# Latent attention in a two-layer decoder: scores made a second time with keys over the partitions, in place of turning the probabilities

## The chip, the cores and the metric

The kernel runs on one core of a Trainium2 chip. The core has five engines that run side by side and meet only at semaphores: TensorE (PE in the profile; its weight loads are PEld), VectorE (DVE), ScalarE (ACT), GpSimd (POOL) and SyncE (SP), which mostly issues DMAs. Matmuls read SBUF and write PSUM, which has eight banks of 512 float32 per partition. GpSimd works on SBUF here, never on PSUM. The metric is device time of one execution in microseconds (us); lower is better. The whole decoder (two layers) is one program, and the change touches only its first attention.

## What is computed

The part that matters is the self-attention of layer 0, on 2 sequences of 1024 tokens with 256 channels, 16 heads of 16 channels:

```python
q = x @ Wq;  k = x @ Wk;  v = x @ Wv
latent_kv = (k + v) @ W_down_kv              # 64 channels
k_rec, v_rec = latent_kv @ W_up_k, latent_kv @ W_up_v
scores = clip(einsum('bhqd,bhkd->bhqk', qh, kh) / 16, -1e4, 1e4)
scores = clip(scores * exp(-0.0001 * abs(iq - ik)), -1e4, 1e4)
out = einsum('bhqk,bhkd->bhqd', softmax(scores), vh) @ Wo
```

Everything else (a layer norm ahead of each block, cross-attention, a ternary feed-forward block, a linear attention, a second cross-attention and a mixture of experts) stays as it is.

## The kernel before, in words

The program is a row of blocks. Each block gives every engine its list of instructions, and no engine goes on to the next block before all engines and the queues that they fed are through the present one. Two blocks are touched.

`latent_projections` (from L302) makes 16 pieces: for each group of 512 tokens (`g`, four of them) two pieces of queries and two of keys, each 128 channels by 512 tokens. So that bf16 matmuls give float32 scores, each piece is split into three bf16 parts. ScalarE rounds it (L422, first part), VectorE subtracts that (L383, the rest), ScalarE rounds the rest (L429), VectorE subtracts again (L390, third part). VectorE also takes the largest absolute value (L385), from which `k.inside` says whether the clip can be left out. SP stores the three parts to DRAM in one DMA of 384 KB a piece (L445), in `q_parts` and `k_parts`. ScalarE also copies the values to `v_heads` (L433).

`latent_attention` (from L451) goes through 32 pairs of batch and head with 8 query tiles of 128 each, 256 steps in all. SP fetches 12 pieces of 32 KB for each pair (L537, L541) and stacks them to 96 rows: the six products of parts that count, 16 channels each. One step is, for 128 queries:

- TensorE makes the scores of 128 queries by 1024 keys, two matmuls (L578).
- VectorE multiplies them with the fading, writes `probs` and takes the row's peak, in one instruction (L659).
- GpSimd turns the peak's sign (L563), and ScalarE takes the exponential with that as bias and sums the row (L706).
- TensorE turns the 128 x 1024 probabilities, eight transposes (L588), since the product with the values wants keys over the partitions; ScalarE copies three of each four halves out of PSUM (L521), VectorE the fourth (L519).
- TensorE sums over the values (L603): every four steps 64 matmuls of 128 columns, four query tiles side by side in the four column groups of 32. A short chain (L695, L612, L637, L640) turns the result back and divides it by the row sum.

The order is written out by hand: `step` on each engine says what it does in step `s`, with the transposes three steps (`LAG`) and the sums up to eight steps (`TRAIL`) behind. The two score tiles of PSUM banks 0 to 3 alternate, banks 4 and 5 take the transposes, bank 6 the sums, bank 7 what is turned back. The engines run this in loops with registers (`Fori`). At the end of its list GpSimd clears the slots of the mixture of experts: a memset and one DMA of 5031 KB to DRAM (L114, L116).

`cross_attention` (from L733), which is not changed, already works with keys over the partitions, and its rows are used below: scores twice (L826 for the peaks, L851 for the exponential), the peak taken off by a matmul with rows of minus one (L857), the sum over the values with 512 moving columns in four column groups (L871).

## Time and profile before

| | us |
|---|---|
| median of 3 runs | 1614.19 |
| lowest and highest of them | 1610.89, 1617.33 |
| the profiled execution, its own time | 1615.76 |
| its span, first to last instruction | 1614.2 |
| busy in the span: PE, DVE, ACT, POOL | 1340.0, 919.8, 930.1, 190.5 |

The profiled execution is 0.1% above the median. Rows below have their stage or line with them. A row of the timeline gives the start in us, how long the row's instructions took together, the engine, the line and operation, and in brackets how long the engine was idle ahead of it and what released it. Two instructions that follow each other overlap in their latency, so the step from one start to the next is the price of one in a stream, and the mean duration of one is more than that. The granted clock of TensorE is given as a share of 2.4 GHz: 1.00 is the higher of its two levels, 0.50 the lower (1.2 GHz).

### The profile page before, as it was taken

The numbers are of one execution on the slowest core, as the hardware profiler recorded it, in microseconds if no ns is written. First come the engines' busy times: TensorE is split into PE (matmuls) and PEld (weight loads), VectorE is DVE, ScalarE is ACT, GpSimd is POOL, SyncE is SP. The second block draws the span as 40 slices with busy tenths as digits, with TensorE's granted clock in tenths as the row PEclk, the third lists the DMA queues.
The fourth block names the chain that finished last, engine by engine and source line by source line (L and its number), as shares of the span: only waits on it lengthen the run. The fifth ranks groups of instructions, "written<-read, shape, count | busy, mean of one in ns | idle before, by whom it ended". The sixth has DMA issues, their size and how long they took to land. (4 is left out here: it accounts for less than half of the span.)

```text
span 1614.2 us, 36474 instructions
## 1 busy us (share of the span) xinstructions
PE 1340.0 (83%) x12288; PEld 960.2 (59%) x12291; DVE 919.8 (57%) x2059; ACT 930.1 (58%) x1793; POOL 190.5 (12%) x546
## 2 busy tenths in 40 slices
PE   5879999999999995898365699889874489999992
PEld 2347777777777774544223464364354279999992
DVE  5558888888888873532788844563354223323233
ACT  2469999999999991355375377624631033333330
POOL 0001111111111110111200000031120701111110
PEclk9879999999999997899756899988995589999996
DMA  3311010010101013200000100033006211111115
GB/s 115 131 51 31 22 27 24 24 26 23 29 20 29 20 38 110 80 1 4 16 1 0 31 1 1 1 120 129 1 4 212 102 34 36 37 36 38 36 33 166
DMA packets 60025, 74.30 MB, mean 46 GB/s; under 512 B 13006, under 2 KB 47728, under 8 KB 59952
## 3 DMA queue, kind: packets, MB, share of 16 engines
q1 hardware_dynamic: 53168, 56.76, 11.9%
q0 software_dynamic: 4672, 14.50, 2.7%
q10 hardware_dynamic: 2112, 2.10, 0.4%
q8 instruction: 43, 0.70, 0.2%
q14 instruction: 30, 0.25, 0.0%
HBM read 50.43 MB, written 22.88 MB: 45 GB/s over the span
## 5 line engine op out<-in xcount | busy, mean ns | idle before, releaser
L659 DVE CUSTOM_DVE_ANT_0 probs_sb<-banks,decay_sb 128x1024 f32<-128x1024 f32 x256 | 308.2, 1221 | 43.6 <-PE banks L578 22.5
L706 ACT ACTIVATE probs_sb<-probs_sb,shift_sb 128x1024 f32<-128x1024 f32 x256 | 294.8, 1151 | 18.1 <-POOL shift_sb L563 16.4
L588 PEld LDWEIGHTS banks<-ident_sb,probs_sb 128*128 128x128 f32 x2048 | 238.3, 141 | 55.1 <-issue 22.9
L588 PE MATMUL banks<-ident_sb,probs_sb 128*128 128x128 f32 x2048 | 267.8, 274 | 0.9 <-ACT probs_t_sb L521 0.8
L521 ACT ACTIVATE probs_t_sb<-banks 128x512 f32<-128x512 f32 x384 | 214.7, 597 | 4.1 <-PE banks L588 2.3
L578 PE MATMUL banks<-k_stack_sb,q_stack_sb 96*128 96x512 bf16 x512 | 156.9, 389 | 14.0 <-DMA k_stack_sb<-k_parts 10.7
L603 PE MATMUL banks<-probs_t_sb,v_head_sb 128*32 128x128 f32 x4096 | 151.2, 277 | 0.7 <-ACT probs_t_sb L521 0.7
L1846 PEld LDWEIGHTS banks<-slots_xt_sb,tile_w_sb 128*128 128x128 f32 x1248 | 146.5, 193 | 1.9
L1846 PE MATMUL banks<-slots_xt_sb,tile_w_sb 128*128 128x128 f32 x1248 | 146.6, 276 | 0.0
L1858 PE MATMUL banks<-experts_w_sb,xt_sb 128*128 x624 | 141.2, 379 | 1.3 <-issue 1.3
L1892 ACT ACTIVATE slots_xt_sb<-banks 128x256 f32<-128x256 f32 x39 | 14.9, 383 | 213.8 <-PE banks L1832 213.8
L1858 PEld LDWEIGHTS banks<-experts_w_sb,xt_sb 128*128 128x128 f32 x624 | 115.5, 190 | 15.8 <-issue 1.7
L519 DVE COPY probs_t_sb<-banks 128x512 f32<-128x512 f32 x128 | 88.6, 692 | 57.7 <-PE banks L588 56.0
L603 PEld LDWEIGHTS banks<-probs_t_sb,v_head_sb 128*32 128x32 f32 x4096 | 100.3, 109 | 32.3 <-issue 31.4
L563 POOL TENSOR_TENSOR shift_sb<-peak_sb,minus_sb 128x1 f32<-128x1 f32 x256 | 48.5, 190 | 452.8 <-DVE peak_sb L659 452.8
L977 DVE TENSOR_REDUCE peak_sb<-banks 128x8 f32<-128x616 f32 x64 | 49.9, 798 | 87.8 <-PE banks L826 87.8
L1019 ACT ACTIVATE pt_sb<-banks,keyfill_sb 77x1024 f32<-77x1024 f32 x64 | 67.5, 1104 | 38.0 <-PE banks L857 37.1
L1902 ACT ACTIVATE xt_sb<-banks,tile_b_sb 128x128 f32<-128x128 f32 x312 | 84.7, 387 | 5.1 <-PE banks L1846 3.4
L1942 DVE COPY tile_w_sb<-experts_w_sb 128x2048 f32 x39 | 47.8, 1227 | 60.2 <-issue 28.0
L1927 DVE TENSOR_TENSOR is_best_sb<-slots_x_sb,tile_owned_sb 128x1 f32<-128x1 f32 x39 | 6.2, 159 | 122.2 <-DMA outputs_y<-slots_y_sb,output_row_sb 122.2
L253 POOL TENSOR_TENSOR x_sb<-x_sb,bb_sb 128x256 f32<-128x256 f32 x48 | 33.0, 732 | 337.2 <-DMA bb_sb<-in_L_attn_bo 276.7
L1881 POOL DMA_INDIRECT outputs_y<-slots_y_sb,output_row_sb x39 | 37.4, 959 | 258.7 <-DVE slots_y_sb L1955 154.0
(289 smaller groups left out, 1910.0 us busy)
## 6 DMA issues: line engine op xcount, KB each, us to landing
experts_w_sb<-in_L_ffn_W SPq DMA_DIRECT2D x16, 1024.0 KB, 11.9
q_stack_sb<-q_parts SPq DMA_DIRECT2D x192, 32.0 KB, 1.7
k_stack_sb<-k_parts SPq DMA_DIRECT2D x192, 32.0 KB, 1.8
slots_x<-zeros_sb POOLq DMA_DIRECT2D x1, 5031.0 KB, 22.6
slots_x_sb<-slots_x SPq DMA_DIRECT2D x39, 129.0 KB, 2.1
xt_sb<-outputs_y SPq DMA_DIRECT2D x8, 512.0 KB, 5.5
q_parts<-parts_sb SPq DMA_DIRECT2D x8, 384.0 KB, 3.0
k_parts<-parts_sb SPq DMA_DIRECT2D x8, 384.0 KB, 4.2
```

The source lines that it names most:

```text
L519: ins = eng.tensor_copy(dst, k.ps[:, 4 + half, :])
L521: ins = eng.activation(dst, k.ps[:, 4 + half, :], ACT.Copy)
L578: last = pe.matmul(k.ps[:, 2 * (s % 2) + half, :], qs[:, u, q * P:(q + 1) * P], ks[:, u, half * 512:(half + 1) * 512], start=True, stop=True)
L588: last = pe.transpose(k.ps[:, 4 + half, j * P:(j + 1) * P], pr[:, s % 4, (half * TPG + j) * P:(half * TPG + j + 1) * P], k.ident[:, :])
L603: last = pe.matmul(k.ps[32 * j:32 * j + 32, 6, 0:P], vh[:, u, kt, :], pt[:, j, gs % 2, kt, :], start=kt == 0, stop=kt == QT - 1)
L659: dve.tensor_tensor_reduce(out=pr[:, s % 4, :], in0=scores, in1=decay[:, off:off + S], scale=1.0, scalar=-3.0e38, op0=ALU.mult, op1=ALU.ma ...
L706: act.activation(pr[:, s % 4, :], pr[:, s % 4, :], ACT.Exp, bias=shift[:, s % 8:s % 8 + 1], accum_out=sums[:, (s // TPG) % 4, s % 4:s % 4 ...
L977: dve.tensor_reduce(peak[:, t % TPG, 2 * half:2 * half + 2, :], k.ps[:, bank:bank + 2, 0:SLOTS * C].rearrange("p r (s n) -> p r s n", n=C) ...
L1019: act.activation(pt[:, n % 2, 2 * half:2 * half + 2, :], k.ps[0:C, 2 * half:2 * half + 2, :], ACT.Exp, bias=key_fill[:, b:b + 1]).then_inc ...
L1846: last = pe.matmul(k.ps[:, 2 * u + f // HALF, (f % HALF) * P:(f % HALF + 1) * P], w1[:, u, kd, f * P:(f + 1) * P], xst[:, u, kd, :], start ...
L1858: last = pe.matmul(k.ps[:, 6, s * D:(s + 1) * D], ht[:, s, f, :], r.w2[:, bass.ds(e, 1), f, :].rearrange("p a n -> p (a n)"), start=f == 0 ...
L1902: ins = act.activation(ht[:, s, f, :], k.ps[:, 2 * s + f // HALF, (f % HALF) * P:(f % HALF + 1) * P], ACT.Gelu_apprx_tanh, bias=b1[:, s, f ...
```

## The change

In the projections every query and key piece is made in two versions: multiplied along the token with exp(-0.0001 i) or exp(+0.0001 i), and the second version negated twice (the sign is in both queries and keys). The fading exp(-0.0001 |i - j|) is then part of the product: one version holds for keys up to the query, the other for keys after it. So there are 32 pieces to split and store where there were 16, the fading being one VectorE instruction with the maximum in it; the third part moves to GpSimd. The value matmuls go behind the queries of the next group, and the queries of group 0 ahead of the latent weights. Six slots hold parts where there were four. Two fade tables (512 KB each), a second table `inner` beside `decay` and rows of minus one are fetched by DMA in this block.

The stacks in SBUF are laid out anew: channel c of piece x lies on partition 6c + x, and four heads are fetched by one DMA (6 of 128 KB of queries for every group, 6 of 256 KB of keys for every second). Rows 96 to 98 of the key stack are minus one, and those of the query stack get the peaks, in three bf16 parts, by DMA.

The attention goes through 16 groups of 4 heads by 512 queries. Each group has 16 tiles of 128 queries by 1024 keys, whose scores serve only for the peak (VectorE, one instruction a tile, result thrown away), and 8 steps over tiles of 128 keys. A step makes for each of the four heads the scores of 128 keys by 512 queries with the peak taken off, and ScalarE takes their exponential from PSUM into the layout that the sum over values wants. Where a key tile lies on the diagonal (4 of 8 steps) a fifth unit makes the four diagonal blocks in the other version, and GpSimd zeroes in both what does not hold (`affine_select`, two a step). The sum over values follows two steps behind. The row sum comes from a column of ones in `v_head`. The transposes, their copies, the sign on GpSimd and the loops with registers are gone; the order is unrolled.

```diff
-                for half in range(2):
-                    last = pe.matmul(k.ps[:, 2 * (s % 2) + half, :], qs[:, u, q * P:(q + 1) * P],
-                                     ks[:, u, half * 512:(half + 1) * 512], start=True, stop=True)
+                for version in range(2):
+                    for half in range(2):
+                        lo, hi = max(half * G, 0 if version == 0 else edge), min((half + 1) * G, edge if version == 0 else S)
+                        if lo < hi:
+                            last = pe.matmul(k.ps[:, 2 * (tile % 2) + half, lo - half * G:hi - half * G],
+                                             stacks.q[0:ROWS, g % 3, version, h, j * P:(j + 1) * P],
+                                             stacks.k[0:ROWS, g // 2 % 2, version, h, lo:hi], start=True, stop=True)
...
+            def key_product(g, i, h, bank, version, lo, hi, at):
+                kt = key_tile(g, i)
+                return pe.matmul(k.ps[:, bank, at:at + hi - lo],
+                                 stacks.k[0:ROWS + PARTS, g // 2 % 2, version, h, kt * P:(kt + 1) * P],
+                                 stacks.q[0:ROWS + PARTS, g % 3, version, h, lo:hi], start=True, stop=True)
...
-            def turn(i, s):
...
+                if on_diagonal(i):
+                    pe.wait_ge(selected, s // 2 + 1)
+                    lo = block_of(g, i) * P
+                    for h in range(HEADS):
+                        pe.matmul(k.ps[VW * h:VW * (h + 1), PV_BANK, lo:lo + P], vh[:, n % 2, h, kt, :],
+                                  probs_d[:, s // 2 % 2, h, :], start=False, stop=False, skip_group_check=True)
+                for h in range(HEADS):
+                    last = pe.matmul(k.ps[VW * h:VW * (h + 1), PV_BANK, :], vh[:, n % 2, h, kt, :], probs_of(s)[:, h, :],
+                                     start=i == 0, stop=i == QT - 1, skip_group_check=True)
...
+            for tile in range(TILES + LEAD):
+                scores(tile)
+                if tile == TILES + 1:
+                    turn_peaks(0)
+            for g in range(GROUPS):
+                for i in range(QT):
+                    if g * QT + i >= 2:
+                        sum_values(g * QT + i - 2)
+                    for x in range(2):
+                        for h in range(2 * x, 2 * x + 2):
+                            key_scores(g, i, h)
+                        if x == 1 and i == TURN_STEP and g + 1 < GROUPS:
+                            turn_peaks(g + 1)
+                        if tile_at(g, i, x) < GROUPS * TILES:
+                            scores(tile_at(g, i, x))
+                    if on_diagonal(i):
+                        diagonal_scores(g, i)
+                    if i == 3 and g > 0:
+                        turn_mix(g - 1)
...
+                pool.wait_ge(exp_done, unit_index(g, i, HEADS - 1) + 1)
+                pool.affine_select(later, later, [[0, HEADS], [1, P]], ALU.is_ge, 0.0, base=0, channel_multiplier=-1)
+                earlier = probs_d[:, s // 2 % 2, :, :]
+                pool.wait_ge(exp_done, unit_index(g, i, HEADS) + 1)
+                pool.affine_select(earlier, earlier, [[0, HEADS], [-1, P]], ALU.is_gt, 0.0, base=0,
+                                   channel_multiplier=1).then_inc(selected, 1)
...
+            def exponential(g, i, h):
+                u, s = unit_index(g, i, h), g * QT + i
+                act.wait_ge(key_scored, u + 1)
+                act.wait_ge(released, u + 1)
+                if h == 0:
+                    wait(act, summed, s - 2)
...
+                act.activation(out, k.ps[:, bank_of((exp_done, u + 1)), :], ACT.Exp).then_inc(exp_done, 1)
```

The key scores, the turned peaks and what is turned back share banks 4 to 6 in a ring (`bank_of`, `wait_for_bank`): an item waits until the third before it has been read. `LEAD` is 6, `TILES` 16, `TURN_STEP` 5, `UNITS` 36 a group, so that 22 tiles go ahead of the first key scores. In the projections:

```diff
+                dve.tensor_tensor_reduce(out=rest[:, e % 4, :], in0=k.ps[:, n % 4, :], in1=fade[:, side, half * G:(half + 1) * G],
+                                         scale=sign * (scale if is_query(e) else 1.0), scalar=-3.0e38, op0=ALU.mult, op1=ALU.max,
+                                         accum_out=extremes[:, version, n:n + 1]).then_inc(faded, 1)
+            def subtract_first(e):
+                dve.wait_ge(part1_done, e + 1)
+                dve.tensor_tensor(rest[:, e % 4, :], rest[:, e % 4, :], parts[:, e % SLOTS, 0, :],
+                                  ALU.subtract).then_inc(rest1_done, 1)
...
+        @block.gpsimd
+        def _(pool):
+            for e in range(NV):
+                pool.wait_ge(part2_done, e + 1)
+                pool.wait_ge(rest1_done, e + 1)
+                pool.tensor_tensor(parts[:, e % SLOTS, 2, :], rest[:, e % 4, :], parts[:, e % SLOTS, 1, :],
+                                   ALU.subtract).then_inc(part3_done, 1)
```

`clear_slots` stays the last thing on GpSimd's list in the attention.

## Rows read from the trace of the kernel before

**Rows 1.** Busy time by stage: projections, attention.
```profile
core 0: us, PE busy (x) PEld busy (x) DVE busy (x) ACT busy (x) POOL busy (x), PEclk, DMA share, GB/s
22.50:84.00 61.50, 48.26 (x106) 20.25 (x106) 31.61 (x55) 25.43 (x53) 0.00 (x0) 0.81 0.31 103
84.00:621.50 537.50, 510.11 (x6720) 375.91 (x6720) 412.60 (x768) 498.26 (x961) 59.75 (x292) 0.97 0.13 33
```

**Rows 2.** Groups of instructions in the attention: busy us, mean ns, idle before.
```profile
L706 ACT ACTIVATE probs_sb<-probs_sb,shift_sb 128x1024 f32<-128x1024 f32 x256 | 294.8, 1151 | 18.1 <-POOL shift_sb L563 16.4
L521 ACT ACTIVATE probs_t_sb<-banks 128x512 f32<-128x512 f32 x384 | 214.7, 597 | 4.1 <-PE banks L588 2.3
```

**Rows 3.** Timeline of the attention's end, DVE, PE and POOL.
```profile
607.51 0.22 DVE L640 TENSOR_TENSOR attn_sb<-banks,inv_sb 128x64 f32<-128x64 f32 x1 [3.04 <-PE banks L612]
622.23 0.45 PE L261 MATMUL banks<-ident_sb,attn_sb 128*128 128x128 f32 x1 [14.82 <-PEq L475]
...
599.24 2.22 POOL L116 DMA_DIRECT2D slots_x<-zeros_sb  x1 [0.32 <-POOL zeros_sb L114]
```

**Rows 4.** DMA issues: size and median us from issue to landing.
```profile
slots_x<-zeros_sb POOLq DMA_DIRECT2D x1, 5031.0 KB, 22.6
q_stack_sb<-q_parts SPq DMA_DIRECT2D x192, 32.0 KB, 1.7
f_b_sb<-in_L_ffn_b SPq DMA_DIRECT2D x1, 512.0 KB, 3.4
```

**Rows 5.** Groups of instructions in the projections.
```profile
L383 DVE SCALAR_TENSOR_TENSOR rest_sb<-banks,parts_sb 128x512 f32<-128x512 f32 x16 | 11.0, 686 | 22.0 <-ACT parts_sb L422 22.0
L429 ACT ACTIVATE parts_sb<-rest_sb 128x512 bf16<-128x512 f32 x16 | 8.7, 617 | 0.0
```

**Rows 6.** GpSimd elementwise groups anywhere in the program.
```profile
L253 POOL TENSOR_TENSOR x_sb<-x_sb,bb_sb 128x256 f32<-128x256 f32 x48 | 33.0, 732 | 337.2 <-DMA bb_sb<-in_L_attn_bo 276.7 <-DMA bb_sb<-in_L_xattn_bo 60.5
L563 POOL TENSOR_TENSOR shift_sb<-peak_sb,minus_sb 128x1 f32<-128x1 f32 x256 | 48.5, 190 | 452.8 <-DVE peak_sb L659 452.8
L559 POOL COPY v_head_sb<-v_heads_sb 128x128 f32<-128x128 f32 x4 | 1.2, 289 | 0.1
L548 POOL MEMSET v_head_sb<- 128x512 f32 x1 | 0.5, 524 | 84.9 <-issue 84.9
```

**Rows 7.** The stretch of 40 to 44 us: DMA at full load, stores of four pieces.
```profile
40.00:44.00 4.00, 4.00 (x7) 2.13 (x8) 0.50 (x1) 0.82 (x3) 0.00 (x0) 0.50 1.03 340
```

**Rows 8.** Timeline of the attention's start.
```profile
85.33 0.52 POOL L548 MEMSET v_head_sb<- 128x512 f32 x1 [84.88 <-issue]
90.91 1.89 PE L578 MATMUL banks<-k_stack_sb,q_stack_sb 96*128 96x512 bf16 x4 [10.71 <-DMA k_stack_sb<-k_parts]
92.11 1.23 DVE L659 CUSTOM_DVE_ANT_0 probs_sb<-banks,decay_sb 128x1024 f32<-128x1024 f32 x1 [11.11 <-PE banks L578]
93.26 1.22 DVE L659 CUSTOM_DVE_ANT_0 probs_sb<-banks,decay_sb 128x1024 f32<-128x1024 f32 x1
```

**Rows 9.** PE's timeline over one and a half steps in mid-attention.
```profile
303.35 0.60 PE L578 MATMUL banks<-k_stack_sb,q_stack_sb 96*128 96x512 bf16 x2
303.78 1.04 PE L588 MATMUL banks<-ident_sb,probs_sb 128*128 128x128 f32 x8
304.75 0.86 PE L603 MATMUL banks<-probs_t_sb,v_head_sb 128*32 128x128 f32 x24
305.55 0.60 PE L578 MATMUL banks<-k_stack_sb,q_stack_sb 96*128 96x512 bf16 x2
```

**Rows 10.** Timeline of the first cross-attention: value sum and exponentials.
```profile
685.59 1.07 PE L871 MATMUL banks<-pt_sb,va_sb 77*32 77x512 f32 x8
691.01 2.11 ACT L1019 ACTIVATE pt_sb<-banks,keyfill_sb 77x1024 f32<-77x1024 f32 x2 [0.48 <-PE banks L857]
```

**Rows 11.** PE's clock while the attention gets going.
```profile
99.00:100.00 1.00, 1.00 (x6) 0.80 (x5) 1.00 (x2) 0.52 (x2) 0.00 (x0) 0.50 0.00 0
100.00:200.00 100.00, 98.94 (x1286) 73.11 (x1284) 80.59 (x149) 97.11 (x188) 11.03 (x56) 1.00 0.10 25
```

More of the change, by code:

```diff
@@ L341, in latent, with values @@
                 last.then_inc(lat_ready, 1)
-            latent(0)
+            def values(g, m):
+                for t in range(g * TPG + 2 * m, g * TPG + 2 * m + 2):
+                    wait(pe, v_done, t - 1)
+                    pe.matmul(k.ps[:, 5 + t % 2, 0:D], lat[:, t * P:(t + 1) * P], k.wuv[:, :],
+                              start=True, stop=True).then_inc(v_ready, 1)
             for g in range(NG):
@@ L347, in _ @@
                     n = 4 * g + m
[L348 removed]
+                    if g > 0:
+                        values(g - 1, m)
+                    wait(pe, faded, 2 * (n - 3))
                     for kd in range(KD):
@@ L360, in _ @@
                     latent(g + 1)
[L361 to L365 removed]
+            for m in range(KD):
+                values(NG - 1, m)
             pe.wait_ge(largest_ready, 1)
@@ L440, in _ @@
+            later.start(sp)
+            for e in range(NV):
+                n, version = divmod(e, 2)
                 g, s = divmod(n, 4)
@@ new lines, in _, with load_stacks @@
+                if 20 <= e < 26:
+                    load_stacks(sp, stacks, 0, e - 20)
+            for x in range(SLOTS):
+                sp.wait_ge(stored[x], 16 * len(range(x, NV, SLOTS)))
+            later.wait(sp)
+class Stacks:
+    pass
+HEADS = 4
+def load_stacks(eng, stacks, g, piece):
+    n, half = divmod(g, 2)
+    b, first = divmod(n * HEADS, H)
+    rows = slice(b * D + first * HD, b * D + (first + HEADS) * HD)
+    q_part, k_part = [(0, 0), (0, 1), (0, 2), (1, 0), (1, 1), (2, 0)][piece]
+    dst = slice(piece, 6 * HD, 6)
+    if half == 0:
+        eng.dma_start(stacks.k[dst, n % 2, :, :, :].rearrange("p v h n -> p v (h n)"),
+                      stacks.k_scratch[:, k_part, rows, :].rearrange("v (p h) n -> p v (h n)", h=HEADS)
+                      ).then_inc(stacks.arrived[g % 3], 16)
+    eng.dma_start(stacks.q[dst, g % 3, :, :, :].rearrange("p v h n -> p v (h n)"),
+                  stacks.q_scratch[:, q_part, half, rows, :].rearrange("v (p h) n -> p v (h n)", h=HEADS)
+                  ).then_inc(stacks.arrived[g % 3], 16)
@@ new lines, in _ @@
+            own.wait()
+            stage_values(0)
+            split_peaks(0)
+            for g in range(GROUPS):
+                for i in range(QT):
+                    if on_diagonal(i):
+                        select(g, i)
+                    if i == 3 and g % 2 == 0 and g + 2 < GROUPS:
+                        stage_values(g // 2 + 1)
+                    if i == TURN_STEP - 1 and g + 1 < GROUPS:
+                        split_peaks(g + 1)
+            clear_slots(k, pool, zeros_set)
```

662 lines of the change are left out of this document (384 added, 278 removed).

## The prediction

> **What bounds it now.** I read the busy time by stage first. The attention takes 537.5 us of the span, the projections ahead of it 61.5. In the attention PE shows 510 us busy, ACT 498, DVE 413 [rows 1]. PE's figure overstates: its rows hold latency, and two score matmuls that show 0.60 us together are followed 0.43 later by the next ones [rows 9], so some 0.17 of each row is latency. The groups then say what ACT does for one step: an exponential of 1024 columns (1.15) and one and a half copies of 512 (0.60 each) [rows 2]: 2.05 us. The 256 steps go from 90.9 to 607.5 [rows 3, 8], 2.02 us each. So ACT sets the pace, and what the change takes from it is the copies.
>
> The timeline of the end shows something else. The last VectorE result of the attention starts at 607.5, and the next block's first matmul at 622.2. GpSimd has issued the clearing DMA at 599.2, which takes 22.6 us [rows 3, 4]: it lands at 621.8. The block cannot end before GpSimd's queue is through, so 14.8 us are idle, and the attention's end is "GpSimd's list is done, plus 22.6 + 0.6". That decides what the new order is worth.
>
> **Projections.** Removed: 16 absolute maxima on DVE. Added: 16 more pieces. For each of the 32, DVE does one multiply-reduce from PSUM and one subtraction, 0.69 each in the row of L383, some 0.6 in a stream: 1.25 us. ACT does two roundings (0.62 each, about 0.55 in a stream) plus values, about 1.3 us [rows 5]. GpSimd's third part is not in the trace at this size. 256 columns with two inputs take 0.73, one column 0.19 [rows 6], hence (0.73 - 0.19) x 2 + 0.19 = 1.27 for 512; the ends are 0.52 (the memset of 512) and 1.46 (twice the 256). It waits for ACT each time, another 0.16 or so. I take the upper end, 1.46 + 0.16 = 1.62 us a piece, since it is GpSimd's only two-input rate here; 32 x 1.62 = 52 us. Fade tables of 512 KB take 3.4 to land [rows 4], so the first piece starts at about 26.5 (22.5 + two issues + 3.4); with 5 us for the last piece and its store the block ends at 83. DMA is close behind: 32 x 384 KB, 1024 + 2016 KB of tables and 2304 KB of the first stacks are 18.1 MB, at the 340 GB/s of a full stretch [rows 7] 53 us. The reorder of values and queries hides under both. So the attention starts at 84, as now. Cover gone: each 0.1 us a piece is 3 us.
>
> **Lead.** GpSimd, from 85.3, first clears 2048 columns (four times 0.52) and copies the identity (0.29) [rows 6, 8], and PE waits for that: first tile at 87.7. Nothing waits for stacks, which now costs 7 us (first matmul at 90.9 though SP starts fetching at 84) [rows 8]. Then 22 tiles pass before the first key scores. VectorE paces them: 1.15 from start to start [rows 8]. The matmuls of tile 21 wait for the reduction of tile 19, at 88.9 + 20 x 1.15 = 111.9. The peaks of group 0 are complete at 107.3, need four small GpSimd steps (0.2 to 0.3 each with their waits), a turn and copy (1.0) and a small DMA (1.7 plus issue), about 111.7: equal. First key scores at 112.3; today the first probabilities come at 93.6. This is a cost of 19 us.
>
> **Main part.** Two steps (one diagonal) are the unit, 64 of them. PE:
> - Value sums: 8 matmuls of 512 columns in column groups take 1.07 with latency [rows 10], 0.90 without. Going in and out costs more: 303.78 + (1.04 - 0.17) is 304.65 and L603 starts at 304.75; 304.75 + 0.69 is 305.44 and L578 starts at 305.55 [rows 9]. So 0.90 + 0.21, twice: 2.22.
> - Diagonal sums: 8 of 128 columns, a third of 0.69: 0.23.
> - Key scores: 8 x 512 columns at 0.215 [rows 9]: 1.72. The three rows more on the contracting side I take as free, since the price is by moving columns in every row here.
> - Peak tiles: 4 x 0.43 = 1.72. Diagonal scores: 512 columns in four matmuls, 0.24. Six matmuls cut in two at the edge: 0.02 each, 0.12.
> - Sum 6.25; 0.05 for the ring of three banks makes 6.3.
>
> Once a group come the turned peaks and four transposes, 0.6 x 16 = 9.6 us; the last 11 steps have no tiles, 22 x 0.43 = 9.5 back. They cancel.
>
> ACT: 9 exponentials of 512. Half of the 1024-column pair's 2.11 / 2 is 0.53 [rows 10], the 512 copy is 0.60 [rows 2]; 0.57 x 9 + 0.25 for peaks and mix = 5.4. DVE: 4 x 1.15 + 0.2 = 4.8. PE becomes the bound, at 6.3 per pair against today's 2.02 x 4 = 8.1 for the same 4 tiles. Low end 5.6 (gaps and ring hidden, ACT next), high end 7.1 (below).
>
> The selects stand on PE's way: the diagonal sum waits for them. By laying out the pair, the fourth exponential of a diagonal step ends at 3.8 us, both selects at 3.8 + 2d + 0.1, and PE wants the result at 5.9; so nothing up to d = 1.0 us, then 2d - 2.0 a pair. The trace has no select. Nearest is the strided copy: 128 columns 0.29, so (0.29 - 0.10) x 4 + 0.10 = 0.86 for 512; the ends are 0.52 (memset) and 1.46 (two inputs) [rows 6]. I take 0.86, no wait; 1.46 would add 0.9 a pair, hence 7.1.
>
> The Trainium skill (GPSIMD Engine Reference, "Elementwise — side-by-side cycle accounting") gives a loop of one input about 1.0 to 1.8 cycles an element, 2.6 with two inputs. By it a select of 512 would be about 0.4 to 0.8 us plus dispatch, an estimate, and would not stall; no run here shows one.
>
> Stacks: 2304 KB every second group, asked for at its start, wanted 5 steps (15.7 us) later; at 340 GB/s 7 us plus 12 issues. Hidden. The queue of SP holds nothing that they delay but the peak rows, wanted three steps later.
>
> PE is at 0.50 through the lead, as it still is at 99 to 100 today [rows 11]; 3 us for the climb. Main part: 64 x 6.3 + 3 = 406, so PE's last diagonal product is at 518.
>
> **Tail.** Exponential and latency 1.0, second select 0.9, then memset and start 0.6 and the DMA's 22.6, 0.3 to the next block: 25.4, so the next block starts at 543.7 instead of 622.2. The remaining sums, about 4 us, lie under that DMA. It is 19 us of idle time instead of 14.8.
>
> **Sum.** Against the profiled 1615.8: -78.5, gives 1537.3; against the median (1614.2) 1536. I say 1537.
>
> **Rivals.**
> 1. *The drains and the ring cost nothing, ACT sets the pace.* 5.6 a pair: 64 x 0.7 = 45 less, 1492. For: from the scores to L588 (303.35 to 303.78) there is no gap. Against: L603 has one of 0.1 on either side [rows 9], and the change keeps its column groups.
> 2. *GpSimd and VectorE exclude each other in the projections.* If the third part (two SBUF inputs) and VectorE's subtraction (two SBUF inputs) take turns, a piece costs 1.62 + 0.69 = 2.31, 32 x 0.69 = 22 us more: 1559. The trace has no such pair of operations together, so it speaks neither way. The Trainium skill (SBUF — State Buffer, "SBUF: two separate sides") states exactly this lock: one blocks the other for a whole instruction.
> 3. *The select is the bound; the one on the other side.* Above 1.0 us each select pushes the diagonal sum, with all of PE's list behind it. At 1.46: 58 us more, 1595. No gain is left at 2d - 2.0 = 78.5 / 64, d = 1.61; slower than before by over 0.5% (1624) from d = 1.68. For: a select also computes an index and a comparison for every element. Against: it has one input, like the copy.
> 4. *The clipped path runs*, because the bound got stricter by exp(-0.2) = 0.82. Over 2000 VectorE instructions more of some 0.6 us: above 2500. The trace shows L659 reading the banks directly [rows 8], which is the unclipped form, with scores of order one against 10000. Practically excluded.
>
> **Chances.** Forecast 0.50 (range of its own 1515 to 1555), rival 1 0.15, rival 2 0.17, a select between 1.0 and 1.6 us 0.08, one at break-even 0.02, slower 0.08. Range 1490 to 1595: from rival 1 to the high end of the select. Half a per cent (8 us) is about what measurement tells from no change. Faster 0.90, same 0.02, slower 0.08.
>
> **What would show it.** PE steps of 3.0 to 3.3 us with small ACT gaps; no L588 and no copies of L521. The multiply-reduce of the peaks at 1.15 in the lead and spaced afterwards. First exponential near 112. GpSimd selects near 0.9 us, and PE's sum never waiting for them. Projections of 32 pieces at 1.6, ending at 83. PE idle for about 19 us at the end under the 22.6 us DMA. Wrong would be: an attention paced by GpSimd, a wait of PE for the stacks at the sixth step of even groups, or pieces above 2 us.

## The result

| | us |
|---|---|
| kernel before, median of 4 runs on the same chip | 1614.64 (1610.89 to 1617.33) |
| kernel after, median of 4 runs | 1557.85 (1553.99 to 1560.41) |
| ratio, 95% interval | 0.9648, 0.9617 to 0.9679 |
| profiled execution of after: own time, span | 1560.41, 1558.3 |

Forecast were 1537 and 1490 to 1595. The time lies in that range but above the forecast's own range of 1515 to 1555. The program became 3.5% faster, 71% of what was forecast: 55.4 us between the two profiled executions where I had 78.5.

**Stages of after** [rows 1], here with the lead as a stage of its own: projections, lead, main part.

```profile
22.50:95.50 73.00, 48.47 (x106) 18.15 (x104) 49.13 (x103) 43.84 (x84) 46.42 (x32) 0.78 0.74 248
95.50:127.00 31.50, 23.12 (x64) 5.91 (x65) 25.13 (x43) 1.56 (x2) 3.81 (x8) 0.50 0.41 101
127.00:538.00 411.00, 400.33 (x3185) 163.04 (x3184) 289.52 (x500) 305.24 (x603) 95.13 (x193) 0.99 0.21 50
```

The projections take 73 us where they took 61.5. In the main part PE is busy for 97% of the time at a clock of 0.99, ACT for 74%, DVE for 70%. ACT's copies are gone, and the bound has moved to PE.

**PE, ACT and DVE in mid-attention** [rows 9], the weight loads left out:

```profile
303.82 0.60 PE L654 MATMUL banks<-q_stack_sb,k_stack_sb 99*128 99x512 bf16 x2
...
304.16 1.23 DVE L816 CUSTOM_DVE_ANT_0 faded_scores_sb<-banks,inner_sb 128x1024 f32<-128x1024 f32 x1 [0.96 <-PE banks L647]
304.26 0.60 PE L647 MATMUL banks<-k_stack_sb,q_stack_sb 96*128 96x512 bf16 x2
...
304.78 0.43 PE L692 MATMUL banks<-probs_d_sb,v_head_sb 128*32 128x128 f32 x8
...
305.02 1.04 PE L695 MATMUL banks<-probs_sb,v_head_sb 128*32 128x512 f32 x8
...
306.00 0.61 PE L654 MATMUL banks<-q_stack_sb,k_stack_sb 99*128 99x384 bf16 x4
...
306.43 1.08 ACT L915 ACTIVATE xt_sb<-banks 128x512 f32<-128x512 f32 x2 [0.99 <-PE banks L654]
```

DVE and ACT both wait about 1 us for PE, once a step; PE has no wait in brackets; over the whole main part its waits come to 8 us. Two score matmuls that start at 304.26 should be through 0.43 later, at 304.69, and L692 starts at 304.78. L695 starts at 305.02, has 0.87 of columns, and L654 follows at 306.00 instead of 305.89. These are the gaps of 0.09 and 0.11 around work in column groups. The next L692 is at 310.91, so a pair of steps takes 6.13 us.

**Groups that carry the attention and the projections** [rows 2, 5, 6]: busy us, mean ns, idle before.

```profile
L915 ACT ACTIVATE xt_sb<-banks 128x512 f32<-128x512 f32 x342 | 178.0, 604 | 73.4 <-PE banks L654 73.4
L775 POOL TENSOR_SCALAR_AFFINE_SELECT probs_d_sb<-probs_d_sb 128x512 f32<-128x512 f32 x63 | 40.0, 634 | 2.2 <-ACT probs_d_sb L915 2.0
L703 PE MATMUL banks<-ident_b_sb,peak_parts_sb 128*96 128x128 bf16 x15 | 3.9, 257 | 4.7 <-POOL peak_parts_sb L764 4.7
...
L439 POOL TENSOR_TENSOR parts_sb<-rest_sb,parts_sb 128x512 bf16<-128x512 f32 x32 | 46.4, 1477 | 44.3 <-ACT parts_sb L455 44.2
L405 DVE TENSOR_TENSOR rest_sb<-rest_sb,parts_sb 128x512 f32<-128x512 f32 x32 | 29.4, 919 | 8.2 <-ACT parts_sb L451 8.1
L399 DVE CUSTOM_DVE_ANT_0 rest_sb<-banks,fade_sb 128x512 f32<-128x512 f32 x32 | 21.7, 681 | 10.8 <-DMA fade_sb<-in_c_fade 5.5 <-PE banks L376 5.3
```

L405 is the same subtraction as L383 before, which took 686 ns; here its mean is 919.

**The attention's start and end** [rows 3, 8]:

```profile
99.06 0.29 POOL L744 CAST ident_b_sb<-ident_sb 128x128 bf16<-128x128 f32 x1
...
99.41 1.89 PE L647 MATMUL banks<-k_stack_sb,q_stack_sb 96*128 96x128 bf16 x6 [9.38 <-POOL ident_b_sb L744]
...
100.59 1.23 DVE L816 CUSTOM_DVE_ANT_0 faded_scores_sb<-banks,inner_sb 128x1024 f32<-128x1024 f32 x1 [9.17 <-PE banks L647]
...
539.99 0.63 POOL L775 TENSOR_SCALAR_AFFINE_SELECT probs_d_sb<-probs_d_sb 128x512 f32<-128x512 f32 x1
540.57 0.31 POOL L114 MEMSET zeros_sb<- 128x258 f32 x1
540.77 0.42 PE L692 MATMUL banks<-probs_d_sb,v_head_sb 128*32 128x128 f32 x8 [0.97 <-POOL probs_d_sb L775]
...
541.20 2.23 POOL L116 DMA_DIRECT2D slots_x<-zeros_sb  x1 [0.32 <-POOL zeros_sb L114]
...
543.75 0.43 DVE L800 TENSOR_TENSOR attn_sb<-banks,inv_sb 128x256 f32<-128x256 f32 x1
563.38 3.01 PE L261 MATMUL banks<-ident_sb,attn_sb 128*128 128x128 f32 x13 [19.96 <-PEq L590]
```

DVE has its last result at 544.2, and the next block begins at 563.4, after 19 us under the clearing DMA.

**DMA issues** [rows 4]:

```profile
k_stack_sb<-k_parts SPq DMA_DIRECT2D x48, 256.0 KB, 4.9
q_stack_sb<-q_parts SPq DMA_DIRECT2D x96, 128.0 KB, 3.4
...
slots_x<-zeros_sb POOLq DMA_DIRECT2D x1, 5031.0 KB, 21.8
```

So the 58.8 us by which the next block begins earlier (622.2 before) are made of a first key or score product 35.5 later (90.9 to 126.4), 104.4 less from there to the last diagonal product or DVE result (516.6 to 412.2), and 10.1 more of tail (14.7 to 24.8). The rest of the program, the same code, took 3.5 us longer in this execution. That ACT set the pace before is read from its rows [rows 1, 2]; no run changes the copies alone.

### The profile page after: what moved, and what is told of

Its sections match the earlier page's. It is cut to its first block and busy times, and to the rows that moved or that the text cites. A ratio compares the mean times of both kernels' runs of the same rounds, so it can differ in the third digit from the quotient of the medians.

```text
span 1558.3 us, 26085 instructions
## 1 busy us (share of the span) xinstructions
PE 1257.4 (81%) x8850; PEld 752.1 (48%) x8851; DVE 840.2 (54%) x1883; ACT 759.1 (49%) x1473; POOL 279.8 (18%) x491
## 2 busy tenths in 40 slices
DMA packets 63104, 96.09 MB, mean 62 GB/s; under 512 B 11057, under 2 KB 51923, under 8 KB 61459
## 3 DMA queue, kind: packets, MB, share of 16 engines
q1 hardware_dynamic: 56214, 78.14, 17.1%
## 5 line engine op out<-in xcount | busy, mean ns | idle before, releaser
L816 DVE CUSTOM_DVE_ANT_0 faded_scores_sb<-banks,inner_sb 128x1024 f32<-128x1024 f32 x256 | 304.5, 1223 | 102.2 <-PE banks L647 101.1
L915 ACT ACTIVATE xt_sb<-banks 128x512 f32<-128x512 f32 x344 | 179.0, 604 | 73.4 <-PE banks L654 73.4
L654 PE MATMUL banks<-q_stack_sb,k_stack_sb 99*128 99x128 bf16 (+3 forms) x960 | 181.0, 297 | 5.8 <-ACT xt_sb L915 2.6
L647 PE MATMUL banks<-k_stack_sb,q_stack_sb 96*128 96x512 bf16 (+3 forms) x704 | 163.9, 339 | 13.7 <-POOL ident_b_sb L744 9.4
L654 PEld LDWEIGHTS banks<-q_stack_sb,k_stack_sb 99*128 99x128 bf16 x960 | 71.7, 97 | 158.9 <-ACT xt_sb L915 66.6
L915 ACT ACTIVATE probs_sb<-banks 128x512 f32<-128x512 f32 x168 | 87.3, 605 | 34.2 <-PE banks L654 34.2
L647 PEld LDWEIGHTS banks<-k_stack_sb,q_stack_sb 96*128 96x128 bf16 x704 | 66.0, 101 | 75.8 <-DVE peak_sb L816 16.8
L695 PE MATMUL banks<-xt_sb,v_head_sb 128*32 128x512 f32 x688 | 90.6, 598 | 0.0
L772 POOL TENSOR_SCALAR_AFFINE_SELECT xt_sb<-xt_sb 128x512 f32<-128x512 f32 x43 | 27.3, 635 | 182.0 <-ACT xt_sb L915 182.0
L293 DVE TENSOR_TENSOR x_sb<-x_sb,banks 128x256 f32<-128x256 f32 x64 | 26.9, 421 | 52.6 <-PE banks L275 35.8
```

What stands on the lines that cost most here:

```text
L647: last = pe.matmul(k.ps[:, 2 * (tile % 2) + half, lo - half * G:hi - half * G], stacks.q[0:ROWS, g % 3, version, h, j * P:(j + 1) * P], st ...
L654: return pe.matmul(k.ps[:, bank, at:at + hi - lo], stacks.k[0:ROWS + PARTS, g // 2 % 2, version, h, kt * P:(kt + 1) * P], stacks.q[0:ROWS ...
L695: last = pe.matmul(k.ps[VW * h:VW * (h + 1), PV_BANK, :], vh[:, n % 2, h, kt, :], probs_of(s)[:, h, :], start=i == 0, stop=i == QT - 1, sk ...
L816: dve.tensor_tensor_reduce(out=junk[:, tile % 2, :], in0=tile_scores(tile), in1=inner[:, window(tile)], scale=1.0, scalar=-3.0e38, op0=ALU ...
L915: act.activation(out, k.ps[:, bank_of((exp_done, u + 1)), :], ACT.Exp).then_inc(exp_done, 1)
```

## The experiments

Twelve kernels ran, each against the kernel before on the same chip. Times in brackets are the lowest and highest, the ratio is to the kernel before. They ran on four chips, where the median of the kernel before was 1611.83, 1612.66, 1612.93 and 1615.62 us, and after ran beside 1614.64. A difference from after of 2 or 3 us can therefore be the chip's, and the ratios decide.

**Where the tail goes.** On the kernel after, the slots are cleared behind group 8.

```diff
+                if g == CLEAR_GROUP:
+                    clear_slots(k, pool, zeros_set)
-            clear_slots(k, pool, zeros_set)
```

> The changed kernel with clear_slots issued after group 8 of the 16, not at the end of GpSimd's list. Theory A (the attention block ends when GpSimd's 5031 KB DMA has landed): the 19.6 us from the last VectorE result (544.2) to the next block's first matmul (563.4) shrink to 1 to 2 us, less one pause of 2.2 us at most in the middle: 1538 to 1541 us. Rival (the block's end waits for something else, or the DMA in the middle slows the fetches of the stacks so that TensorE waits for them): 1550 or more, or a wait for the stacks of several us in groups 9 and 10.

Measured: 1544.07 us (1543.21 to 1547.2), ratio 0.9585 [0.9564, 0.9606], 13.8 less than after, and 10 less by the ratios: above theory's 1538 to 1541, well below the rival's 1550. In the trace the next block begins 16.3 earlier:

```profile
543.83 0.42 DVE L802 TENSOR_TENSOR attn_sb<-banks,inv_sb 128x256 f32<-128x256 f32 x1
547.05 2.37 PE L261 MATMUL banks<-ident_sb,attn_sb 128*128 128x128 f32 x10 [3.55 <-PEq L591]
```

The 19 us are 2.8, and the DMA beside the groups slows none of them: every group from the third to the thirteenth takes 26.02 us, as in after. The same edit on the kernel before, with the clearing behind the first pass:

```diff
-            bodies(pool, body)
+            body(0, True, False)
             clear_slots(k, pool, zeros_set)
+            with pool.Fori(1, NB - 1) as i:
+                body(i, False, False)
+            body(NB - 1, False, True)
```

> The kernel before with the same move: clear_slots after the first unrolled pass (step 16) instead of at the end. Theory A: the 14.8 us of idle time at the attention's end go, and GpSimd's 2.2 us of issuing delay the sign of one peak once: 1600 to 1603 us. The difference of the two kernels without the tail is then 60 to 63 us, against 57 with it. Rival: the DMA collides with the small stack fetches in the loop: over 1608.

Measured: 1602.95 us (1602.46 to 1603.73), ratio 0.9947 [0.993, 0.9965]. That lies in theory's 1600 to 1603, but against 1611.83 on this chip it is 8.9 less, where 14.8 less a pause of 2.2 was expected. In the trace the next block begins 12.5 earlier (609.75), after 3.0 us idle. Without either tail the two kernels differ by 58.9 us, with both by 56.8; 60 to 63 was expected.

**Is the select near PE's path?** Every select is done twice.

```diff
+                own.did(pool.affine_select(later, later, [[0, HEADS], [1, P]], ALU.is_ge, 0.0, base=0, channel_multiplier=-1))
+                own.wait()
                 pool.affine_select(later, later, [[0, HEADS], [1, P]], ALU.is_ge, 0.0, base=0, channel_multiplier=-1)
...
```

> The changed kernel with every affine_select on GpSimd done twice (the second changes nothing). One select took 0.635 us here, so two count as d = 1.27 to 1.35 with the wait between. Theory (the layout of the prediction: free up to d = 1.0, then 2d - 2.0 a pair of steps): 0.55 to 0.7 us a pair, 64 pairs, 35 to 45 us more: 1593 to 1603. Rival (more slack than laid out, since the sum over a diagonal tile follows a whole step later and TensorE is the bound): under 15 us more. Other rival (GpSimd's selects slow VectorE or ScalarE by themselves): more than 60, with longer single operations.

Measured: 1574.51 us (1573.78 to 1579.92), ratio 0.9781 [0.9756, 0.9806]; theory's 1593 to 1603 is missed, and the rival's limit of 15 more is passed by little. The main part, first exponential to last key product, went from 410.8 to 429.3 us: 18.5 more, 0.29 a pair. From start to start a doubled select takes 1.29, and my layout of the pair gives 2 x 1.29 - 2.0 = 0.58, 37 us. So the rule "free up to 1.0, then twice the excess" is too strict: if its slope holds, which one point can't show, the free part ends at 1.15. As the select takes 0.635 there is room of some 0.5 us for each, and it costs nothing. The stalls are in half of the pairs only, in PE's waits (us in total, times, longest):

```profile
PE banks L692 <- POOL probs_d_sb L780: 15.9, 33, 1.0
```

**The extra step of a group.** A group of 8 steps takes 26.02 us where 8 x 3.07 are 24.56. One of the steps with extras is the one that turns the next group's peaks (3.62), where PE waits 0.31 for GpSimd. First, split and turn both go one step later.

```diff
-    TURN_STEP = 5
+    TURN_STEP = 6
```

> The changed kernel with TURN_STEP 6 for 5: the peaks of the next group are split and turned one step later. In the profile a group takes 26.02 us against 8 x 3.07 = 24.56; 0.54 of the excess is TensorE's wait for the split peaks in the sixth step. Theory B: that wait goes, 15 x 0.5 = 7 to 8 us less: 1550. Rival: the peak rows then arrive too late at the next group's first key scores (turn, copy and DMA of about 3 us in 2 steps), so the wait only moves: 1556 to 1560 or more.

Measured: 1558.09 us (1555.53 to 1559.09), ratio 0.9671 [0.9654, 0.9688], as the rival said. PE still waits, 0.37 us now, and the step takes 3.71. The wait had only moved along, since GpSimd's split had moved too. Then the turn alone goes later, and the split stays:

```diff
-    TURN_STEP = 5
+    TURN_STEP = 6
...
-                    if i == TURN_STEP - 1 and g + 1 < GROUPS:
+                    if i == TURN_STEP - 2 and g + 1 < GROUPS:
                         split_peaks(g + 1)
```

> Against the kernel after: GpSimd still splits the peaks of the next group after step 4, TensorE turns them one step later (6 instead of 5). In the earlier run with both moved, TensorE still waited 0.37 us for GpSimd in that step. Theory: the wait of 0.31 us and what hangs on it (the step at 3.62 instead of 3.07) is GpSimd's chain of four small operations behind the last tile's peak; a step of distance takes all of it: the step goes from 3.6 to 3.1 to 3.3, 15 groups by 0.3 to 0.5 are 5 to 8 us, time 1550 to 1553. Rival: what the step costs is the turn itself (four transposes, a bank of the ring held, a copy), so it only moves to the next step: 1557 to 1559, spacings as before in another place.

Measured: 1554.31 us (1550.65 to 1557.83), ratio 0.9634 [0.9614, 0.9655], an interval that overlaps that of after, between theory (1550 to 1553) and rival (1557 to 1559). PE at the turn:

```profile
278.29 0.23 PE L703 MATMUL banks<-ident_b_sb,peak_parts_sb 128*96 128x128 bf16 x1 [0.18 <-ACT xt_sb L915]
```

GpSimd's chain is off the path; in its place comes 0.18 of wait for ACT, which must empty the bank of the ring that the turn wants. The main part is 2.6 us shorter, 0.17 a group: the step goes from 3.62 to 3.49, not to 3.1. So the bulk of the 0.54 is the turn itself and its bank, which this run does not separate.

**The first pieces.** PE waits for the latent weights from 26.5 to 31.8, since DVE copies them only behind two pieces, and those wait for the fade tables. The copy goes ahead of that wait.

```diff
+            dve.wait_ge(wkv_ready, 1)
+            dve.tensor_copy(wkv[:, :, :], k.ps[:, 7, 0:KD * L]...).then_inc(wkv_done, 1)
             dve.wait_ge(fade_arrived, 2 * 16)
...
```

> The changed kernel, where VectorE copies the combined latent weights (0.28 us) ahead of its wait for the fade tables, not after its third fade. In the profile TensorE sits idle from 26.5 to 31.8 for that copy, and VectorE later waits 5.3 us for the first keys and ACT 3.8 for the first values. Theory C: the attention starts 4 to 8 us earlier (at 88 to 92 for 95.5): 1550 to 1554. Rival (the block ends with the DMA traffic, 18 MB at 340 GB/s, which runs at full load from 76 to 92 whatever the start): start at 94 or later, no gain beyond 1.5 us.

Measured: 1556.29 us (1556.11 to 1559.65), ratio 0.9662 [0.9635, 0.9689], not told from after; theory's 1550 to 1554 is missed. The trace's next block starts 2.5 us earlier. PE's wait of 5.3 us for the weights is gone, but its first key product now waits 5.4 us for ACT's copy of the latent, which stands behind the fourth piece on ACT's list.

**GpSimd against VectorE.** The third part goes back to VectorE.

```diff
+            def subtract_second(e):
+                dve.wait_ge(part2_done, e + 1)
+                dve.tensor_tensor(parts[:, e % SLOTS, 2, :], rest[:, e % 4, :], parts[:, e % SLOTS, 1, :],
+                                  ALU.subtract).then_inc(part3_done, 1)
...
-        @block.gpsimd
...
```

> The changed kernel with the third part subtracted on VectorE as in the kernel before, not on GpSimd. In the profile VectorE's subtraction of two SBUF inputs took 1.03 us beside a GpSimd subtraction and 0.69 when alone, GpSimd's 1.48 beside it and 1.15 alone; a piece took 1.57. Theory D (the two share access to SBUF): the subtractions on VectorE are back at 0.69 in every row, and a piece takes 0.61 + 0.60 + 0.60 = 1.8 to 1.9: the start of the attention moves by 0 to +8 us. Rival (VectorE's rows were long for another reason, such as waiting for parts): they stay near 1.03 for the first subtraction, and a piece takes 2.2 or more.

Measured: 1559.65 us (1559.01 to 1561.67), ratio 0.9678 [0.9652, 0.9704]. VectorE's two subtractions a piece:

```profile
L405 DVE TENSOR_TENSOR rest_sb<-rest_sb,parts_sb 128x512 f32<-128x512 f32 x32 | 21.9, 683 | 0.6 <-ACT parts_sb L450 0.5
L410 DVE TENSOR_TENSOR parts_sb<-rest_sb,parts_sb 128x512 bf16<-128x512 f32 x32 | 21.8, 681 | 0.1
```

Alone, the subtraction is at 683 ns again instead of 919, so the conflict is real. In after the two engines' subtractions look like this, in the steady part and at the end, where they hardly overlap:

```profile
52.77 1.04 DVE L405 TENSOR_TENSOR rest_sb<-rest_sb,parts_sb 128x512 f32<-128x512 f32 x1
53.22 1.60 POOL L439 TENSOR_TENSOR parts_sb<-rest_sb,parts_sb 128x512 bf16<-128x512 f32 x1
54.34 1.04 DVE L405 TENSOR_TENSOR rest_sb<-rest_sb,parts_sb 128x512 f32<-128x512 f32 x1
...
81.62 0.69 DVE L405 TENSOR_TENSOR rest_sb<-rest_sb,parts_sb 128x512 f32<-128x512 f32 x1 [0.58 <-ACT parts_sb L451]
82.18 1.15 POOL L439 TENSOR_TENSOR parts_sb<-rest_sb,parts_sb 128x512 bf16<-128x512 f32 x1 [0.74 <-ACT parts_sb L455]
```

That fits two engines that take turns. VectorE alone has a price of 0.61 from start to start; GpSimd's 1.15 less the 0.19 of an operation on one column [rows 6] leaves 0.96 for the elements; together 1.57, an estimate from these rows, and a piece takes 1.57. The rows overlap all the same, as a row is longer than its price in a stream (0.69 for 0.61). No run separates this from a slowdown of another kind.

What GpSimd's help is worth, the medians don't tell. VectorE alone makes a piece in 1.81 us (from 43.1 to 68.5 us), as theory said, and with the help in 1.57. That is 0.25 a piece. But the trace of this run had luck with PE's clock while the pipe filled (below, at the step that failed), and after had not. Beside the three traces with the third part on GpSimd and the same luck, `select_twice`, `turn_step_6` and `rows_two_halves`, VectorE's last piece begins 4.6 to 7.4 us later (87.26 for 79.83 to 82.68), and GpSimd's first memset of the attention comes 2.7 to 5.7 later (98.23 for 92.53 to 95.52).

**The first stacks.** They are fetched in the attention and not beside the last pieces.

```diff
-                if e == 19:
-                    for x in range(SLOTS):
-                        sp.wait_ge(stored[x], 16 * len(range(x, 16, SLOTS)))
-                if 20 <= e < 26:
-                    load_stacks(sp, stacks, 0, e - 20)
...
-            for g in range(1, 3):
+            for g in range(3):
```

> The changed kernel with the first group's stacks fetched at the start of the attention, not between the stores of the projections. Theory E (the end of the projections is bound by DMA: the stores and 2304 KB of fetches share the queue from 72 on, and pieces take 2.3 us instead of 1.57 from 78 to 91): the projections end 6 to 8 us earlier, and the fetch, now in the open, costs about 9: near 0, 1555 to 1562. Rival (the slow pieces at the end have another cause): the projections end where they do, at 91 to 95, and the fetch adds 7 to 9 us: 1564 or more.

Measured: 1564.28 us (1561.85 to 1566.54), ratio 0.97 [0.9674, 0.9726]. GpSimd's first memset of the attention comes at 94.6 instead of 97.2, so without the fetches the projections are 2.6 shorter, but the first tile waits for the stacks until 106.7. Theory's 6 to 8 us did not come out, and the time is the rival's. Both edits together:

> Against the kernel after: the latent weights are copied ahead of the wait for the fade tables, and the first group's stacks are fetched in the attention. Singly the first shortened the projections by 2.4 us of the 5.3 that VectorE had waited (DMA was full from 72 to 88), the second brought GpSimd's first memset of the attention from 97.2 to 94.6. Theory: the copy's gain was lost to the DMA queue, so without the stack fetches the whole 5 us come out: memset at 89 to 90.5, first tile some 12 us behind it, time 1558 to 1561 (5 less than with stacks late alone, 1564.3). Rival: the pace of the 32 pieces on GpSimd and VectorE ends the block either way: memset at 92.5 or later, 1562 to 1565.

Measured: 1564.38 us (1560.4 to 1565.4), ratio 0.969 [0.9674, 0.9706]; the memset is at 91.85, 2.7 earlier than with stacks late alone, where theory said 5 and the rival 2. Of these, 1.1 lie ahead of the block, whose first matmul comes at 21.86 instead of 23.01. The medians do not show even the rest. The copy therefore did not lose its gain to DMA. What took the place of the wait is seen in VectorE's list:

```profile
36.20 0.69 DVE L399 CUSTOM_DVE_ANT_0 rest_sb<-banks,fade_sb 128x512 f32<-128x512 f32 x1 [3.44 <-PE banks L376]
...
43.41 0.69 DVE L405 TENSOR_TENSOR rest_sb<-rest_sb,parts_sb 128x512 f32<-128x512 f32 x1 [4.08 <-ACT parts_sb L450]
```

and among the waits of this kernel (us in total, times, longest):

```profile
PE banks L376 <- ACT lat_sb L445: 5.3, 1, 5.3
...
ACT v_heads_sb L459 <- PE banks L355: 4.3, 1, 4.3
```

PE's key product now waits for ACT's copy of the latent, which stands behind the fourth piece on ACT's list (`e == 3`); and ACT stands at a copy of values with the next roundings behind it. The order of the lists makes the hole, not the one copy; and PE's clock was at 0.50 from 34 to 42 us.

**Rows of the stack.** A piece of 16 channels is put on 16 neighbouring partitions instead of six apart; all else stays.

```diff
-    dst = slice(piece, 6 * HD, 6)
+    dst = slice(piece * HD, (piece + 1) * HD)
```

> The changed kernel without the interleaving: each of the six pieces lies on 16 partitions in a row (piece x on 16x to 16x + 15), everything else as it is. Theory F (a fetch of 128 or 256 KB is spread by its source rows, and what it costs lies under the 15 us that a group leaves): landing within 1 us of 3.4 and 4.9, total within 3 us of 1558. Rival (16 neighbouring partitions share few ports into SBUF): landing times 1.5 to 2 times as long, the fetches of an even group take over 15 us, and TensorE waits for stacks in 7 groups: 1575 or more.

Measured: 1610.03 us (1607.76 to 1614.93), ratio 0.9989 [0.9975, 1.0003]. The whole gain is gone. DMA issues of this kernel, and its main wait from 130 to 580 us (total, times, longest):

```profile
k_stack_sb<-k_parts SPq DMA_DIRECT2D x48, 256.0 KB, 11.7
q_stack_sb<-q_parts SPq DMA_DIRECT2D x96, 128.0 KB, 5.6
```

```profile
PE banks L647 <- DMA q_stack_sb<-q_parts: 30.3, 6, 6.0
```

The busy time by stretch of one set of stacks (the last three columns: PE's clock, DMA share, GB/s):

```profile
192.00:196.00 4.00, 3.85 (x35) 1.53 (x38) 3.32 (x7) 3.01 (x7) 0.00 (x0) 1.00 1.10 121
...
208.00:212.00 4.00, 0.21 (x2) 0.21 (x3) 0.00 (x0) 0.00 (x0) 0.15 (x1) 0.95 0.36 37
212.00:216.00 4.00, 4.00 (x23) 1.96 (x21) 2.42 (x4) 1.84 (x4) 0.87 (x2) 0.50 0.02 5
```

The DMA engines are fully busy at 116 to 121 GB/s; in after the same stretch moves 201 to 240. A set of 2304 KB takes about 21 us instead of 12, and PE wants it 18 us after it is asked for. PE's stand of 5 us also takes the clock to 0.50 for the 4 us after it. The first tile is 11 us later, the main part 44 longer, 30 of them in the waits shown. A version between the two, three apart in two halves of 48 partitions:

```diff
+    dst = slice(piece // 3 * 3 * HD + piece % 3, (piece // 3 + 1) * 3 * HD, 3)
```

> The channels of a piece lie 3 partitions apart, pieces 0 to 2 on partitions 0 to 47 and pieces 3 to 5 on 48 to 95, instead of 6 apart over all 96. Landing of a 256 KB piece of keys was 4.9 us with 6 apart and 11.7 with 16 neighbouring partitions. Theory: the landing goes by how far the 16 rows are spread over the partitions, so it is in between, 6 to 9 us; all 2304 KB of a pair of groups are then through in time or just so, and the program takes 1556 to 1575. Rival one: any spacing is enough (no neighbours in a piece): 4.9 us and 1556 to 1560. Rival two: what counts is that all six pieces share the same partitions, so that a transfer reaches everywhere: landing 10 us or more and 1590 or above.

Measured: 1559.19 us (1555.81 to 1561.83), ratio 0.9673 [0.9659, 0.9688]:

```profile
k_stack_sb<-k_parts SPq DMA_DIRECT2D x48, 256.0 KB, 7.8
```

Landing goes 4.9, 7.8, 11.7 with 96, 48 and 16 partitions reached. These medians hold the wait behind the transfers ahead: on 16 partitions the first of a set's six key pieces lands in 4.6 us and the last in 17.1. The middle layout is still hidden. The Trainium skill (SBUF — State Buffer, "Door 1: The DMA port swizzle (why `[64,N]` ≈ `[32,N]`)") counts for this the ports that a transfer's partitions reach: by its table 13 or 14 with six apart, 8 or 12 with three apart, and 4 for 16 neighbours. The order agrees, and its 104 GB/s for partitions 0 to 15 is near the 116 to 121 here; ports as such no run here shows.

**A version that beats both.** The early clearing, the copy first, the later turn, and PE's wait for the identity moved from the first tile to the first turn:

```diff
-            pe.wait_ge(constants, 1)
             for tile in range(TILES + LEAD):
                 scores(tile)
                 if tile == TILES + 1:
+                    pe.wait_ge(constants, 1)
...
```

> Four edits together on the kernel after: the slots are cleared behind group 8 instead of at the end, the latent weights are copied ahead of the wait for the fade tables, TensorE waits for the identity only where it first turns peaks, and the peaks are turned one step after they are split. Singly: clearing early 1544; the copy about -2; the wait for the identity 1.5 to 2.5 at the first tile; the turn 0 or 5 to 8. Theory: they add up, 1532 to 1541. Rival: the head of the attention is set by when the DMA queue is through, so that only clearing and turn count: 1537 to 1545.

Measured: 1535.25 us (1532.21 to 1536.85), ratio 0.9518 [0.9504, 0.9532]; its interval and that of the early clearing alone (0.9564 to 0.9606) do not meet. Theory's sum, 1532 to 1541, holds.

```profile
94.52 1.87 PE L647 MATMUL banks<-k_stack_sb,q_stack_sb 96*128 96x128 bf16 x6 [6.77 <-PEq L322]
```

First tile at 94.5, main part 408.3 us, next block at 539.6. Of the 23.8 us that the next block is earlier than in after, the tail gives 16.4 and the main part 2.5; the other 4.9 lie at the first tile. The wait for the identity explains 3.8 of them: in this trace it is ready at 98.3, and PE starts at 94.5 with the block's first fetch, where in after it started 3.85 behind it. The rest is not told from chance: with no edit in the projections' order the first tile came anywhere from 94.75 to 100.81 in six of these profiles.

## Why the prediction came out 20 us low

Right in its main lines: ACT's copies bounded before, the change takes them off, PE becomes the bound, and GpSimd's DMA ends the block. The next block was forecast at 543.7 and came at 563.4. By the steps:

- **Projections, 84 against 95.6: the step that failed.** "The reorder of values and queries hides under both" was false. The rate came out nearly right, 1.57 a piece against 1.62, but by luck: GpSimd's subtraction is 1.15 alone and not 1.46, and what makes up for it is the conflict with VectorE, which the forecast left to a rival. But the first 5 pieces needed 18.5 us instead of 8.1. I had priced every instruction and never laid out who waits for whom while the pipe fills: the fade tables hold DVE's list, which holds the latent weights, hence the latent, the keys and the values.

```profile
38.38 0.69 DVE L399 CUSTOM_DVE_ANT_0 rest_sb<-banks,fade_sb 128x512 f32<-128x512 f32 x1 [5.29 <-PE banks L376]
...
45.05 0.69 DVE L405 TENSOR_TENSOR rest_sb<-rest_sb,parts_sb 128x512 f32<-128x512 f32 x1 [3.54 <-ACT parts_sb L451]
```

  These two waits of DVE in after are 8.8 of the 11.6. The whole sum: the first piece is 1.7 late (28.2), the first five cost 10.4 more, 0.6 pass before the sixth, the steady rate gives 1.6 back, the last five take 1.7 more since the stores meet the stack fetches (3.9 us of ACT waiting for stores; DMA share 1.05 from 80 to 88), and from the last piece to the block's end it is 4.3 us instead of the 5.7 that the forecast left.

  A part of it is PE's clock, which the forecast had at nothing here. PE stands still from 26.5 to 31.8, the clock falls to 0.50 and stays there to 43, and PE's list of the latent, the keys, the next latent and the values, all ahead of ACT's copy of values, runs at half speed. In `select_twice`, with the same projections, it was back at 1.00 by 36. The second latent in after, and in `select_twice`:

```profile
39.84 3.61 PE L348 MATMUL banks<-xt_sb,wkv_sb 128*64 128x512 f32 x4
...
38.08 1.93 PE L348 MATMUL banks<-xt_sb,wkv_sb 128*64 128x512 f32 x4
```

  From the first latent to the next queries PE takes 12.7 us in after and 9.2 in `select_twice`, and DVE's two waits are 8.83 and 5.35. So 3.5 of the 11.6 are the clock, beside an execution where it rose early. Three of the six profiles went each way: 99.41 to 100.81 at the first tile with the late rise (after, `clear_mid`, `peaks_turned_later`), 94.75 to 97.74 with the early one. What decides between them no run shows. With the early rise the fetches still begin at 90.9 to 93.9 instead of 84, so the waits on the lists remain the larger part.
- **Lead.** "VectorE paces them: 1.15" was the rate of an engine whose input is ready. Reductions start 1.15 and 1.35 apart in turn, 1.25 on average; PE, at 0.50, gives every second tile late. The first key product comes 27.0 behind the first tile instead of 24.6: 2.4 more. So the first exponential, the forecast's sign for this part, is at 127.1 and not near 112.
- **Pair of steps.** 6.13 against 6.3, 11 us less. The terms for columns and for the column groups' gaps stand. The terms without the 0.12 for the splits and the 0.05 for the ring add up to 6.13, so these two did not show.
- **Once a group.** 0.6 was the bare work; measured are 1.46 (26.02 - 8 x 3.07), some 13 us more: 0.6 for turning the mix back, 0.54 for the peaks, 0.3 where ACT copies the mix. The later turn above shows one reason: such a turn holds a bank of the ring of three that ACT must empty first. The last eleven steps without tiles gave back 0.6 a pair, not 1.7: then ACT and the ring set 5.5 us a pair. "They cancel" is off by 19; 11 came back in the pairs and the 3 for the clock were not all needed, so the main part is 6 longer than its 406.
- **Select.** 0.635 measured, 0.86 forecast, free in both; what it would have cost if longer was overestimated, 0.58 a pair against 0.29 at 1.29.
- **Stacks.** "...at 340 GB/s 7 us plus 12 issues. Hidden." It was hidden, but by 6 us and not by 9: the rate was 201 to 240. I had put "hidden" on a transfer without asking how its destination lies; the change's unremarkable slice with step 6 turned out to be worth 52 us.
- **Tail.** 24.8 from the last diagonal product, forecast 25.4.

Of the rivals, the first (ACT paces, 1492) was wrong: both gaps around the column groups are there. The second had the mechanism as far as the rows tell, and the wrong price. The two engines' subtractions lengthen each other, GpSimd's from 1.15 to 1.60 and VectorE's from 0.69 to 1.04, and a piece takes what taking turns gives (the sum of 0.61 and 0.96 above), but that is 1.57 and not the rival's 2.31, so its 22 us are not there, and that it names the measured time (1559) is luck. The Trainium skill (SBUF — State Buffer, "SBUF: two separate sides") states that the one blocks the other for a whole instruction. The rows agree with it, as far as a row without its fixed part is the instruction. The third (a select above 1.6) and the fourth (the clipped path) did not occur.

The 3.5 us of the unchanged rest are not explained. In the spans it is 2.9 (992.0 to 994.9), and in the twelve kernels of the experiments the same stretch takes 991.0 to 995.7.

## What to carry to other kernels

Price the fill of a pipeline by laying out its first pieces on every engine's list: a wait at the head of a list delays everything that stands behind it, and moving one copy only brings up the next wait. Before an edit is given a few us of a trace, read the granted clock of that stretch in several executions: here it cost one execution 3.5 us that another did not pay, as much as the edits of the projections moved. A tail under a DMA at the end of a block costs nearly its full length (16 of 19 us and 12 of 15 in the traces here), and the cure is its place in the list. When a DMA writes few partitions, spread its rows over many before the slots and lead times are tuned.

## What the chip showed that was not expected

- A destination of 16 neighbouring partitions halved the DMA rate, 118 GB/s with all engines busy against about 220 with the same bytes and descriptors six partitions apart (63104 packets in both).
- Two-input operations of GpSimd and VectorE in SBUF lengthen each other, 1.15 to 1.60 us and 0.69 to 1.04 in a stream. The rows overlap, but the pace of 1.57 is that of taking turns with the elements (0.61 and 0.96, an estimate from these rows).
- A select of 128 x 512 takes 0.635 us on GpSimd, about as a memset of that size (0.52) and far below a two-input operation (1.15).
- With the same projections PE's clock was back at 1.00 by 36 us in three profiles and only at 43 or 44 in three others.
- PE stayed at 0.50 for the whole lead and the first 4.6 us of the main part, though its rows show it 27 of 34 us busy, and averaged 0.95 in the 10 us after that:

```profile
97.00:131.00 34.00, 27.12 (x74) 7.43 (x75) 28.18 (x47) 4.21 (x7) 3.81 (x8) 0.50 0.37 93
131.00:141.00 10.00, 10.00 (x77) 4.29 (x75) 7.59 (x14) 7.28 (x15) 2.64 (x5) 0.95 0.00 0
```
